# Attention heads of a mixture-of-experts layer: projections at blocks 2, 4, 6 and 8 with keys first, and products with gates and factors of two pairs on GpSimd

## The reference, cut to what matters

```python
q = (x @ w_q).reshape(b, n, HEADS, DIM_HEAD).transpose(0, 2, 1, 3)
k = (x @ w_k).reshape(b, n, HEADS, DIM_HEAD).transpose(0, 2, 1, 3)
gates = jax.nn.sigmoid((x @ w_gate).reshape(b, n, HEADS, EXPERTS).transpose(0, 2, 1, 3))
sel = jnp.argmax(gates, axis=-1)
gm = jax.nn.one_hot(sel, EXPERTS, dtype=x.dtype) * gates
values = jnp.einsum('bhne,ehdk,bnd->bhnk', gm, value_experts, x)
sim = jnp.einsum('bhid,bhjd->bhij', q * SCALE, k)        # then the causal mask
attn = jax.nn.softmax(sim, axis=-1)
out = jnp.einsum('bhij,bhjk->bhik', attn, values)
out = jnp.einsum('bhne,ehkd,bhnk->bhnd', gm, output_experts, out)
return out.sum(axis=1)
```

## Time and profile before

| | |
|---|---|
| median of 3 runs | 980.87 us (978.87 to 981.49) |
| profiled execution | 981.5 us |
| its span | 979.7 us |
| TensorE busy | 919.9 us, 94% |
| VectorE busy | 655.9 us, 67% |
| GpSimd busy | 399.7 us, 41% |
| ScalarE busy | 344.2 us, 35% |

### The profile page before, as it was taken

One profiled execution on the slowest core, in us unless ns is written; L12 is line 12 of the kernel. 1 busy time (PEld: TensorE's weight loads), 2 busy tenths in 40 slices (PEclk: granted clock), 3 DMA queues, 4 the chain that ended last, 5 costly groups with the idle time before them and its releaser, 6 DMA issues.

```text
span 979.7 us, 15292 instructions
## 1 busy us (share of the span) xinstructions
PE 919.9 (94%) x5740; PEld 704.1 (72%) x5740; DVE 655.9 (67%) x1038; ACT 344.2 (35%) x628; POOL 399.7 (41%) x363
## 2 busy tenths in 40 slices
PE   6989999999998898999999998999999989989998
PEld 3568778887655554699975786888776555549998
DVE  4857566548464668499969666754765565658887
ACT  4635555020354544411124455710104444541000
POOL 6312322213787869547620042300235765773100
PEclk9989999999999999999999999999999999999999
DMA  6103000524253542368530000022321010124863
GB/s 212 49 11 119 2 1 8 167 98 144 67 172 120 163 138 54 101 187 211 173 129 1 1 1 1 1 93 86 97 76 33 12 34 13 44 72 125 191 202 104
DMA packets 52462, 86.06 MB, mean 88 GB/s; under 512 B 11127, under 2 KB 32343, under 8 KB 52391
## 3 DMA queue, kind: packets, MB, share of 16 engines
q1 hardware_dynamic: 51111, 80.91, 27.4%
q10 hardware_dynamic: 1280, 4.20, 1.9%
HBM read 61.39 MB, written 19.33 MB: 82 GB/s over the span
## 4 chain that ended last, share of the span: by engine, by line
PE 78%; DVE 11%; issue 4%; ACT 4%; POOL 1%; DMA 1%; SPq 0%; ACTq 0%; POOLq 0%; DVEq 0%
PE ps L1233 16%; PE ps L1577 11%; PE ps L1500 6%; PE ps L1583 5%; PE ps L1412 5%; PE ps L1241 4%; PE ps L1457 4%; PE ps L1546 3%; PE ps L1364 3%; PE ps L1426 3%; PE ps L1474 3%; PE ps L1379 2%; DVE region L1105 2%; PE ps L1547 2%; PE ps L1510 2%
## 5 line engine op out<-in xcount | busy, mean ns | idle before, releaser
L1105 DVE TENSOR_REDUCE region<-ps 128x1 f32<-128x512 f32 (+1 forms) x192 | 97.6, 550 | 85.4 <-PE ps L1477 79.4
L1577 PE MATMUL ps<-expert_hi,kst 128*128 128x256 f32 x512 | 125.0, 283 | 1.8 <-DVE kst L1179 1.6
L1149 DVE COPY_PREDICATED region<-region,ps 128x512 f32<-128x512 uint32 x112 | 81.9, 735 | 66.6 <-PE ps L1233 66.2
L1577 PE MATMUL ps<-expert_lo,kst 128*128 128x256 f32 x512 | 123.2, 279 | 0.0
L1179 DVE TENSOR_TENSOR kst<-region 128x1024 fp32r<-128x1024 f32 x64 | 84.1, 1314 | 41.0 <-PE ps L1549 21.1
L1233 PE MATMUL ps<-expert_hi,wide_hi 128*128 128x512 f32 x256 | 102.8, 401 | 1.3 <-DVE region L1149 1.3
L642 POOL TENSOR_TENSOR xT<-xT,region 128x896 f32<-128x896 f32 (+2 forms) x48 | 84.3, 1757 | 48.0 <-PE ps L1500 34.2
L1233 PE MATMUL ps<-expert_hi,wide_lo 128*128 128x512 f32 x256 | 100.2, 391 | 0.0
L1233 PE MATMUL ps<-expert_lo,wide_hi 128*128 128x512 f32 x256 | 99.8, 390 | 0.0
L1577 PEld LDWEIGHTS ps<-expert_hi,kst 128*128 128x128 f32 x512 | 96.0, 188 | 5.1 <-issue 4.9
L1577 PEld LDWEIGHTS ps<-expert_lo,kst 128*128 128x128 f32 x512 | 96.5, 188 | 0.0
(11 more groups left out here) (161 smaller groups left out, 1933.6 us busy)
## 6 DMA issues: line engine op xcount, KB each, us to landing
region<-hot_rows SPq DMA_DIRECT2D x128, 128.0 KB, 3.2
halves_kept<-expert_hi SPq DMA_DIRECT2D x16, 512.0 KB, 5.3
halves_kept<-expert_lo SPq DMA_DIRECT2D x16, 512.0 KB, 6.1
expert_hi<-halves_kept SPq DMA_DIRECT2D x64, 128.0 KB, 2.9
expert_lo<-halves_kept SPq DMA_DIRECT2D x64, 128.0 KB, 3.0
expert<-in_value_experts SPq DMA_DIRECT2D x8, 512.0 KB, 4.3
kx<-kst ACTq DMA_DIRECT2D x16, 256.0 KB, 3.0
expert<-in_output_experts SPq DMA_DIRECT2D x8, 512.0 KB, 4.3
```

The lines of the kernel that those rows point to most:

```text
L1105: dve.tensor_reduce(mx[:, i, at_mx:at_mx + 1], ps[:, max_bank(h, m), 0:w], AX.X, ALU.max).then_inc(sem["s_max"], 1)
L1149: dve.copy_predicated(V3_heads[:, t], chosen.unsqueeze(3).broadcast_to([P, PAIRS3, 2, HD3]), ps[:, n % 4, :].rearrange("p (a i k) -> p a i ...
L1577: mm(ps[:, 4 + t // 2, t % 2 * D:(t % 2 + 1) * D], kst[n % 2][:, t * P:(t + 1) * P], w[:, slot, columns], start=(n == 0 and t % 2 == 0 and ...
```

## The change

The projections of a pair move to blocks 2, 4, 6 and 8, keys' two halves first, and each copy to the block of its projection. The copy of the first keys' half waits for the split of the keys before, that of the first queries' half for the other users of the queries. The products with the gates (pair 0 in head 4, pair 1 in head 6) and the gates-times-reciprocal of the factors (heads 3 and 5) go to GpSimd, behind its second addition; the reciprocal stays on VectorE, after maximum m = 4. Pairs 2 and 3 stay on VectorE. The rounding of parts 1 and 3 moves from (5, 6) to (6, 4) and from (7, 2) to (7, 4).

```diff
--- before.py
+++ after.py
@@ -212,7 +212,7 @@
             val_ps=TT * E3, val_a=TT, val_v=TT * (E3 - 1), v3_ready=TT + 1,
             qk_ps=PAIRS3 * 2 * NC, qk_sb=PAIRS3 * 2 * NC,
             qq_ready=H3, qq_twice=H3, kst_ready=2 * H3, qx_ready=H3, o_sb=2 * H3, den_ps=H3, den_sb=H3, summed=H3 * (TT - 1),
-            factors_ready=PAIRS3, o_round=PAIRS3 * NC, o_lo_ready=PAIRS3 * NC,
+            factors_ready=PAIRS3, inverse_ready=PAIRS3, o_round=PAIRS3 * NC, o_lo_ready=PAIRS3 * NC,
             s_ps=H3 * NB, s_max=H3 * NB, tile_max=H3, mxT_ps=H3, m_row=H3,
             st_ps=H3 * NB, pt_ready=H3 * NB, av_used=H3 * TT, oT_ready=PAIRS3 * NC,
             mo_hi_ready=NEP, mo_lo_ready=NEP,
@@ -255,8 +255,10 @@
 
         SPLIT_AT = {(0, 3): 0, (0, 8): 1, (1, 3): 2, (1, 8): 3, (2, 3): 4, (3, 3): 5, (3, 8): 6, (4, 3): 7}
 
-        ROUND_AT = {(5, 4): 0, (5, 6): 1, (7, 1): 2, (7, 2): 3}
-        WEIGHTED_AFTER = 6
+        ROUND_AT = {(5, 4): 0, (6, 4): 1, (7, 1): 2, (7, 4): 3}
+        WEIGHTED_AFTER = 4
+        BY_POOL = 2
+        FACTORS_IN, WEIGHTED_IN = {3: 0, 5: 1}, {4: 0, 6: 1}
         ROUND_LATE_AT = {6: 4, 7: 5, 14: 6, 16: 7}
 
         PARTS = [(p, c * CH, (c + 1) * CH) for p in range(PAIRS3) for c in range(NC)]
@@ -280,8 +282,7 @@
         SCORES = [(t, c) for t in range(TT) for c in range(t // TC + 1)]
         SCORES_AT = {4: (0, 1, 2), 5: (3, 4), 6: (5, 6, 7), 7: (8, 9), 8: (10, 11)}
         MAX_ROW_AT = 10
-        PROJECT_AT = (3, 5, 7, 9)
-        QK_OUT_AT = (4, 6, 8, 10)
+        PROJECT_AT = (2, 4, 6, 8)
 
         BY_SCALAR = 5
         SUM_BANK = (7, 3)
@@ -632,6 +633,24 @@
                                        ALU.subtract).then_inc(sem["o_lo_ready"], 1)
                     until(pool, "o_lo_ready", b, k + 1)
 
+                def times_gates(p):
+
+                    if p == 0:
+                        pool.wait_ge(gate_cols_in, 16 * PAIRS3 * (b + 1))
+                    until(pool, "inverse_ready", b, p + 1)
+                    pool.tensor_tensor(den_cols[:, p % 2, :], den_cols[:, p % 2, :], gate_cols[:, p, :], ALU.mult
+                                       ).then_inc(sem["factors_ready"], 1)
+                    until(pool, "factors_ready", b, p + 1)
+
+                def weighted(k):
+
+                    p, c0, c1 = PARTS[k]
+                    pool.wait_ge(gates_in, 32 * (b * PAIRS3 + p + 1))
+                    until(pool, "o_sb", b, 2 * (2 * p + 2))
+                    pool.tensor_tensor(oT[:, p, c0:c1], oT[:, p, c0:c1], gb[:, c0:c1], ALU.mult
+                                       ).then_inc(sem["oT_ready"], 1)
+                    until(pool, "oT_ready", b, k + 1)
+
                 def add_weights(h, j):
 
                     done = h * (TT - 1) + j - 1
@@ -652,6 +671,11 @@
                             outputs_low(ROUND_AT[h, n])
                         if n in LAST_BLOCK[1:]:
                             add_weights(h, LAST_BLOCK.index(n))
+                        if n == LAST_BLOCK[2] and h in FACTORS_IN:
+                            times_gates(FACTORS_IN[h])
+                        if n == LAST_BLOCK[2] and h in WEIGHTED_IN:
+                            for c in range(NC):
+                                weighted(NC * WEIGHTED_IN[h] + c)
                 for n in range(NEP):
                     if n in ROUND_LATE_AT:
                         outputs_low(ROUND_LATE_AT[n])
@@ -810,10 +834,11 @@
                 copy(gate_T.rearrange("p (i s) -> p i s", i=NC), ps[G:GW, 4:4 + NC, :], "gT_a")
 
                 def qk_evac(p, n):
-                    i, c = n // NC, n % NC
+                    i, c = 1 - n // NC, n % NC
                     until(act, "qk_ps", b, p * 2 * NC + n + 1)
                     if p and n == 0:
                         until(act, "kst_ready", b, 4 * p)
+                    if p and n == NC:
                         until(act, "qx_ready", b, 2 * p)
                         until(act, "qq_twice", b, 2 * p)
                     act.activation(raw[:, i, c * CH:(c + 1) * CH], ps[:, 6, :], ACT.Copy,
@@ -893,8 +918,8 @@
                             den_copy(h - 1)
                         if (h, n) in ROUND_AT:
                             rounded(ROUND_AT[h, n])
-                        if n in QK_OUT_AT and h % 2 == 0 and h + 2 < H3:
-                            qk_evac(h // 2 + 1, QK_OUT_AT.index(n))
+                        if n in PROJECT_AT and h % 2 == 0 and h + 2 < H3:
+                            qk_evac(h // 2 + 1, PROJECT_AT.index(n))
 
                 for i in range(2):
                     output_copy(H3 - 1, i)
@@ -1126,7 +1151,10 @@
                     if p == 0:
                         dve.wait_ge(gate_cols_in, 16 * PAIRS3 * (b + 1))
                     dve.wait_ge(den_in, 16 * (n + 1))
-                    step(dve.reciprocal(den_cols[:, p % 2, :], den_cols[:, p % 2, :]))
+                    dve.reciprocal(den_cols[:, p % 2, :], den_cols[:, p % 2, :]).then_inc(sem["inverse_ready"], 1)
+                    if p < BY_POOL:
+                        return
+                    until(dve, "inverse_ready", b, p + 1)
                     dve.tensor_tensor(den_cols[:, p % 2, :], den_cols[:, p % 2, :], gate_cols[:, p, :], ALU.mult
                                       ).then_inc(sem["factors_ready"], 1)
 
@@ -1160,9 +1188,6 @@
                         split(h)
                     for m in range(NB):
                         maximum(h, m)
-                        if m == WEIGHTED_AFTER and h >= 5 and h % 2:
-                            weighted(h - 5)
-                            weighted(h - 4)
                         if m == WEIGHTED_AFTER and h >= 4 and h % 2 == 0:
                             factors(h // 2 - 2)
                     max_row(h)
@@ -1447,7 +1472,7 @@
 
                 def project(p, n):
 
-                    which, c = n // NC, n % NC
+                    which, c = 1 - n // NC, n % NC
                     until(pe, "qk_sb", b, p * 2 * NC + n)
                     if n == 0 and p:
                         until(pe, "m_row", b, 2 * p - 1)
```

## The result

The changed kernel takes 968.36 us (median of 4 runs, 964.30 to 969.71), the kernel before, run beside it, 981.18 (978.87 to 983.05): ratio 0.9864, interval 0.9827 to 0.9900. It is 12.8 us faster. The forecast was 956.2 with a range of 950.5 to 966.0: the sign is right, the size is half of what was forecast, and the time lies 2.4 us outside the range. The profiled execution took 969.71 us, with a span of 967.9.

What follows compares the result with a forecast made beforehand. TensorE, busy 94% of the span, bounds the kernel through its pauses. Gains of 11.7 and 14.4 us, together 26.1, less tail and split costs, leave 24.7: a median of 956.2 us, range 950.5 to 966.

Steps and rivals of the forecast that it cites:

- What bounds the kernel, and what comes off VectorE: Second item, heads 3, 5 and 6: with products and factors off VectorE, TensorE gains 1.80, 1.26 and 4.53 us.
- the split: VectorE's split for head 6 runs beside GpSimd's later work in head 4: 0.3 us an item, ends 0 and 1.5.
- The projections: Heads 2, 4 and 0 gain 1.46, 2.06 and 0.6 us; first item 2.7 more from waits before L1457.
- The tail: After head 7, part 3's rounding falls behind GpSimd's first sum: costs 0.4 us an item, ends 0 and 1.3.
- I cost the delay at nothing there.: GpSimd's products in heads 4 and 6 delay sums 3 to 7 by 2.6 us; taken to cost nothing.
- 1.05 us of room, and 1.28 us more work.: Head 7's end: room between GpSimd's last sum and its TensorE reader, against the moved rounding; 0.4 us an item taken.
- Rival A: Half-clock stretch at the border of heads 6 and 7 stays: 959.5 us, chance 0.12.
- B: GpSimd becomes what VectorE was: splits delay two heads an item by 1.5 us, tail 1.3; 963.4 us, chance 0.12.
- C: Copies hold ScalarE up: 1.5 us in heads 2 and 4, gain before the transpose gone; 965.8 us, chance 0.06.
- D: Slower: GpSimd waits for the gates' rows ahead of sums 3 to 7, four times 7 us; 984 us, chance 0.03.
- E: Pauses go to the next in line and nothing is gained: 978 to 983.8 us, chance 0.04.
- the bad ends: Upper costs of tail, split and copies: 1.8, 2.4 and 4.8 us on top of 956.2, giving 965.

Runs made afterwards that it cites:

- the projections alone: Kernel before with only the projections' part of the change (blocks 2, 4, 6, 8, keys first, copies in the same block): 972.28 us, ratio 0.9914.
- the late roundings: Changed kernel with parts 2 and 3 rounded after head 7, in the output stage: 959.73 us, ratio 0.9779.

## Why the prediction was right or wrong

**What bounds the kernel, and what comes off VectorE: right.** Item 2, forecast against measured: head 3 1.80 and 1.79, head 5 1.26 and 1.25. Head 6 was 4.53 less 0.3 for the split, and gave 4.12: it is 0.40 longer than its yardstick, head 1. Head 1's length turned out to be the limit, as assumed: 15.62 in heads 3 and 5.

**The projections: right, and a little too low.** Heads 2 and 4 took 20.58 and not 21.37 us, so they gave 2.25 and 2.85 instead of 1.46 and 2.06. The pause that remains in head 1 (15.62 us with 15.09 busy) is gone there (20.58 with 20.56), which the prediction had only as a lower bound; the last 0.3 us say that a projection costs a little less than the 1.44 of the earlier trace rows. Head 0 gave 1.25 where 0.6 was taken. In the first item a new wait of 1.2 us for an exponential (L907) came into head 1, so that it grew from 16.84 to 17.66. Ahead of that exponential ScalarE stood at a piece of the output experts' weights, whose DMA hadn't landed:

```profile
286.02 1.06 ACT L690 ACTIVATE expert_hi<-expert 128x1024 fp32r<-128x1024 f32 x1 [0.72 <-DMA expert<-in_output_experts]
288.00 0.33 PE L1571 MATMUL ps<-qq,kst 128*128 128x128 f32 x1 [1.18 <-ACT region L907]
```

In the kernel before ScalarE didn't wait there. The second item splits no pieces, and has no such wait. In all, the heads gave 28.5 us against a forecast of 26.1 less 0.6. The forecast had the first item ahead by its waits before L1457 (14.4 against 11.7), and it was ahead, but by less: 14.97 against 13.50.

**The tail: the step that failed.** This is the term after head 7 (`denominators` waiting for GpSimd's last sum). The prediction took 0.4 us in each item, with ends 0 and 1.3. Measured: a wait of 5.6 us, 5.25 and 5.34 us of time in head 7. Of the 12.9 us by which the profiled span (down 11.8) misses the forecast (down 24.7), the two tails are 10.6 - 0.8 = 9.8. Two terms went into it wrongly:

- *"I cost the delay at nothing there."* The 2.6 us by which the products push sums 3 to 7 were checked against head 4, with 18 us to the next use. Head 6 was never checked. TensorE passes it 4.1 us sooner now, while GpSimd got 2.6 us of products and 1.28 us of rounding in it, and its queue runs on into head 7 without a gap. "Some backlog from head 6" was in the text, but without a number; it measured 2.3 us, after 5.8 us of former idle time had been used up. Taking either addition out of head 6 (experiments above) took 3.0 and 2.1 us off the wait.
- *"1.05 us of room, and 1.28 us more work."* The work was priced by a rounding with nothing beside it. Beside `masked` it measured 2.17, and sums behind it 0.8 to 0.9 us longer. The earlier trace rows together showed that such a neighbour can double an instruction (2.92 us for two products of 0.69), and this had been used for VectorE's products and splits and not for this place.

**The split: right.** 0.3 us for each item, and head 6 is 0.4 us longer.

**The clock.** Rival A had the half-clock stretch stay at the border of heads 6 and 7. It went from there, with the pause, as the forecast had it. But it reappeared, longer, behind the new wait, 6.8 us in all, of which 4.2 and 4.9 us lie over work. A part of the 4.1 us of the stage between is this.

**The rivals.** B had the right mechanism, GpSimd becoming what VectorE was, but with 1.5 us at the splits, which didn't come, and the tail capped at 1.3; its 963.4 is 5 us short. C's 965.8 is the nearest number, and that is luck: no copy held up TensorE in heads 2 and 4, and the one new wait for an exponential, in head 1, has another cause (above). D didn't happen: L650 took 1.28 us each and no idle time for a DMA stands before it. E neither.

**The range** failed since the tail's upper end was the price of one instruction, and not that of everything that had been added to the same queue. All of it from the rows at hand, 2.6 + 1.28 + 1.28 us less 1.05 of room, is 4.1 us in each item. Put in place of 1.3 in the bad ends, it takes their 965 to 970.6, and the range would have held the time. That sum is still a rough one. It leaves out the 5.8 us of idle time ahead of the first sum and, the other way, the 4.1 us by which TensorE comes sooner and the contention.

**What stays open.** The stage between, 318.29 us in the kernel before, takes 321.05 to 322.54 in all the others, also in the projections alone (321.2), which have head 7 as before. No code of that stage differs. It has two pauses, ahead of L1385 and L1412 (L1410 and L1437 in the kernel after), that are the same in both; the kernel before, and then after:

```profile
549.12 0.83 PE L1385 MATMUL ps<-region,const 128*128 128x2 f32 x6 [0.97 <-DVE region L1026]
550.75 2.00 PE L1412 MATMUL ps<-region 128*128 128x102 f32 x16 [0.79 <-DVE region L1057]
...
543.64 0.83 PE L1410 MATMUL ps<-region,const 128*128 128x2 f32 x6 [0.97 <-DVE region L1051]
545.27 3.04 PE L1437 MATMUL ps<-region 128*128 128x102 f32 x16 [0.80 <-DVE region L1082]
```

Behind the second pause the sixteen products take 2.00 us in one and 3.04 in the other, where the clock is granted at half for 3.4 us: 1.7 us of time. With the 2.1 us behind the tail's wait that is 3.8 of the 4.1 us of the stage. It isn't a tight account: TensorE is busy for 313.42 us in the stage against 310.23, 3.2 more, and 0.9 is new idle time, among it a wait of 1.3 us for `masked`. With the late roundings, where no half-clock stretch follows the tail, the stage still takes 322.46. In the profiled execution of the kernel before this stretch is absent, in all the others it is there, 3.4 or 6.8 us long. Whether the change brings it about by timing, or whether it is chance, wasn't settled; it bears on 1.7 of the 12.9 us. One kernel's own executions differ in this: the fifteen of the kernel before run beside the first experiments have mean granted clocks of 0.988 (984.79 and 985.05 us) to 0.997 (978.11), and 0.996 in the fastest (975.95). The first stage, too, lies between 249.6 and 254.1 us over kernels with the same code in it.

## What to carry to other kernels

When work is moved to an engine that isn't the bound, don't price it at the place where it is put: add up all that is put on that in-order queue, subtract the idle time that it has left up to the next point where the bounding engine reads its result, and do so at the last such point, where no later slack exists. Do the sum with the new, shorter time of the bounding engine, since what is gained ahead of that point is slack lost behind it. At head 6 that was 4.1 us, nearly as much as the work that was added. Here, with the roundings after head 7 and the second pair's products on VectorE the kernel takes 956.06 us, where the forecast had been.

## What the hardware showed that was not expected

- A rounding of 128x512 on GpSimd (1.28 us) beside VectorE's 128x1024 product took 2.17 us in the second item, and the VectorE instruction 2.29 instead of 1.22. Both pay, about 1 us each.
- The clock: behind a pause of 2.2 us the kernel before had 3.3 us at half clock; behind 1.1 us (late roundings) there was none; behind 5.6 us 4.9 and 4.2, after 1.9 and 2.6 already within the pause. But behind the same pause of 2.2 us the projections alone showed over 6 us, and behind the same two pauses of 0.97 and 0.8 us (rows above) one kernel kept its clock and the other lost it. Neither the fall nor its length is told by the pause ahead of it alone.
